# A fourth adding transfer per block in a selective-scan decoder layer, and one product moved from POOL to DVE

## What is computed

```
x = layernorm(x + mamba(x))
x = layernorm(x + cross_attention(x, ctx))
x = layernorm(x + gated_ffn(x))

mamba:  u = silu(conv4(W_in x) + b)           # 1024 channels
        dt, B, C = W_xproj u                  # 16 states
        delta = softplus(W_dt dt + b_dt)
        h_t = exp(delta_t A) h_(t-1) + delta_t B_t u_t   # for each channel and state
        y_t = sum over the 16 states of C_t h_t
        out = W_out ((y + D u) * silu(W_res x))
```

## Time and profile before

| what | value |
|---|---|
| median of 3 runs | 2497.8 us |
| the profiled execution | 2494.77 us |
| its span, first to last instruction | 2493.0 us |
| mamba part in it | up to about 1710 us |
| busy PE, DVE, ACT, POOL, share of the whole span | 93%, 73%, 63%, 67% |
| mean granted TensorE clock | 0.979 |

### The profile page before, as it was taken

One profiled execution on the slowest core, in us unless ns is written; L12 is line 12 of the kernel. 1 busy time (PEld: TensorE's weight loads), 2 busy tenths in 40 slices (PEclk: granted clock), 3 DMA queues, 4 the chain that ended last, 5 costly groups with the idle time before them and its releaser, 6 DMA issues. The chain is left out here.

```text
span 2493.0 us, 38410 instructions
## 1 busy us (share of the span) xinstructions
PE 2328.9 (93%) x15232; PEld 1389.2 (56%) x15232; DVE 1830.0 (73%) x2160; ACT 1566.4 (63%) x2604; POOL 1675.3 (67%) x911
## 2 busy tenths in 40 slices
PE   8898999999999999899999989996799999999997
PEld 4565666566666665566656655563454554554543
DVE  4998898898898899889889878762465366356453
ACT  4786887878888878688788887742333433333332
POOL 1898889899899899789989988871333143143130
PEclk9999999999999999999999999997899999999999
DMA  6677978877878888787787787875000100000000
GB/s 205 142 151 167 223 153 178 216 170 172 219 160 186 207 165 174 163 214 159 168 224 170 167 216 151 209 179 187 1 32 4 34 34 1 34 34 1 17 17 17
DMA packets 104677, 331.67 MB, mean 133 GB/s; under 512 B 9699, under 2 KB 46947, under 8 KB 73779
## 3 DMA queue, kind: packets, MB, share of 16 engines
q0 software_dynamic: 27648, 201.34, 40.9%
q1 hardware_dynamic: 76851, 127.88, 15.1%
HBM read 108.30 MB, written 19.56 MB: 51 GB/s over the span
## 5 line engine op out<-in xcount | busy, mean ns | idle before, releaser
L1028 POOL TENSOR_TENSOR mamba_ring<-mamba_ring,mamba_c_row 128x1024 f32<-128x1024 f32 x512 | 1278.7, 2655 | 39.5 <-DVE mamba_ring L916 39.1
L916 DVE TENSOR_TENSOR_SCAN mamba_ring<-mamba_ring,ps 128x512 f32<-128x512 f32 x1024 | 1175.0, 1200 | 139.8 <-PE ps L456 134.1
L717 ACT ACTIVATE mamba_ring<-mamba_delta,mamba_a_neg 128x512 f32<-128x512 f32 x1024 | 659.4, 710 | 73.5 <-DMA mamba_ring<-mamba_ring 72.1
L456 PEld LDWEIGHTS ps<-shared,mamba_v_t 64*128 64x128 f32 x8192 | 499.5, 189 | 245.1 <-issue 148.1
L456 PE MATMUL ps<-shared,mamba_v_t 64*128 64x128 f32 x8192 | 581.1, 284 | 49.8 <-DVE mamba_ring L916 48.8
L1037 POOL DMA_DIRECT2D mamba_ring<-mamba_ring x192 | 180.3, 939 | 147.6 <-DMA mamba_ring<-mamba_ring 121.8
L1614 POOL TENSOR_TENSOR xf_pr<-xf_pr,xf_top 128x1232 f32<-128x1232 f32 x32 | 75.0, 2344 | 266.4 <-DVE xf_top L1536 266.4
L422 PE MATMUL ps<-mamba_xt,mamba_wres 128*128 128x512 f32 x512 | 239.7, 611 | 0.0
L365 PE MATMUL ps<-mamba_xt,mamba_wu 128*128 128x512 f32 x464 | 218.3, 614 | 5.6 <-DMA mamba_xt<-x_t 5.6
L890 DVE SCALAR_TENSOR_TENSOR mamba_u<-ps,mamba_wcv,mamba_u 128x511 f32<-128x511 f32 (+2 forms) x192 | 142.1, 740 | 74.3 <-ACT mamba_u L682 71.8
L508 PE MATMUL ps<-mamba_wout,mamba_u 128*128 128x512 f32 x352 | 168.0, 611 | 0.3 <-ACT mamba_gate L725 0.3
(11 more groups left out here) (129 smaller groups left out, 2781.7 us busy)
## 6 DMA issues: line engine op xcount, KB each, us to landing
mamba_ring<-mamba_ring POOLq DMA_DIRECT2D x192, 1024.0 KB, 7.7
mamba_c_row<-c_rows SPq DMA_DIRECT2D x32, 1024.0 KB, 11.6
mamba_wres<-w_res SPq DMA_DIRECT2D x64, 256.0 KB, 6.0
mamba_wu<-w_u SPq DMA_DIRECT2D x58, 256.0 KB, 4.0
mamba_xres<-x SPq DMA_DIRECT2D x32, 256.0 KB, 8.9
x<-mamba_xres SPq DMA_DIRECT2D x32, 256.0 KB, 4.4
mamba_xt<-x_t SPq DMA_DIRECT2D x7, 1024.0 KB, 14.2
xf_xn<-x SPq DMA_DIRECT2D x20, 256.0 KB, 4.0
```

Of the source, the lines that this page charges most:

```text
L456: m = nc.tensor.matmul(ps[:, 2 * s + i, tb * P:(tb + 1) * P], v_t[g % 2][i * H:(i + 1) * H, tb * P:(tb + 1) * P], diag_b[i * H:(i + 1) * H ...
L717: a = nc.scalar.activation(ring[:, q % NR, i, :], delta[:, d % EARLY, :], ACT.Exp, scale=a_neg[:, d, 2 * k + i:2 * k + i + 1])
L916: m = nc.vector.tensor_tensor_scan(ring[:, r, i, :], ring[:, r, i, :], both[:, bass.ds(i, T, 2)], 0.0, ALU.mult, ALU.add)
L1028: nc.gpsimd.tensor_tensor(ring[:, q % NR], ring[:, q % NR], c_row[:, 2 * k:2 * k + 2, :], ALU.mult).then_inc(c_done, 1)
```

## The change

A fourth merge of half the size (one slot, 512 KB) adds the slot of step 6 to that of step 7. It is issued after POOL's step 4 of block g + 1 and waits for merge 2. PE's state_sum takes the slot of step 7 alone, and runs at the end of PE's step 7. y_transposes moves to the end of PE's step 0 of block g + 2. v for blocks 6, 7 and the next batch's 0 is made by DVE, behind its scan of step 1 of blocks 5, 6 and 7, and no longer by POOL. ACT's program stays as it is.

```diff
+    LIGHT = 5
-    MERGES = 3
-    SUMS = (6, 7)
+    MERGES = 4
+    SUMS = (7,)
...
     PE step:
-                if k == 6 and g >= 1:
-                    for e in SUMS:
-                        state_sum(g - 1, e)
...
                 if k == 7 and g >= 1:
-                    y_transposes(g - 1)
+                    for e in SUMS:
+                        state_sum(g - 1, e)
+                if k == 0 and g >= 2:
+                    y_transposes(g - 2)
...
+            y_transposes(NG - 2)
...
     DVE:
+            def make_v(g):
+                b, d = g // ND, g % ND
+                dve.wait_ge(delta_ready, g + 1)
+                dve.wait_ge(u_ready, g + 1)
+                dve.wait_ge(vt_proj, g)
+                nc.vector.tensor_tensor(v[:].rearrange("p b i t -> p i b t"), in_blocks(delta[:, d % EARLY, :]),
+                                        in_blocks(u[b % 2][:, d, :]), ALU.mult).then_inc(v_ready, 1)
...
+                if k == 1 and d >= LIGHT and g + 1 < NG:
+                    make_v(g + 1)
...
     POOL merge:
-                src, dst = (g * NU + 2 * p) % NR, (g * NU + 2 * p + 2) % NR
-                pool.wait_ge(c_done, g * NU + 2 * p + 4)
+                n = 2 if p < 3 else 1
+                src, dst = (g * NU + 2 * p) % NR, (g * NU + 2 * p + n) % NR
+                pool.wait_ge(c_done, g * NU + 2 * p + 2 * n)
...
-                nc.gpsimd.dma_start(ring[:, dst:dst + 2], ring[:, src:src + 2], accum_op=ALU.add).then_inc(merged[p], 16)
+                nc.gpsimd.dma_start(ring[:, dst:dst + n], ring[:, src:src + n], accum_op=ALU.add).then_inc(merged[p], 16)
...
     POOL loop:
-                    if k == 0 and g + 1 < NG:
+                    if k == 0 and g % ND < LIGHT:
                         make_v(g + 1)
                     times_c(g * NU + k)
...
                     if k in (3, 6):
                         merge(g, k // 4)
+                    if k == 4 and g >= 1:
+                        merge(g - 1, 3)
             merge(NG - 1, 2)
+            merge(NG - 1, 3)
```

## The result

The changed kernel takes 2768.7 us (median of 4 runs, 2764.8 to 2771.3). The kernel before, on the same chip, takes 2499.1 us. The ratio is 1.109, with a 95% interval of [1.106, 1.111]. So it is 270 us slower. I had said 2640, 142 slower, with 2700 as the upper end: the sign and the place were right, the size was not. In the profiled executions the spans differ by 276.5 us, and the last scan of the mamba part ends at 1940.7 us in place of 1665.4, 275.3 later. What comes behind the mamba part takes 1.2 us more.

A forecast was written before the change was run, and what follows sets the result against it. PE was taken as nearest to a bound, with DVE and ACT as late in some blocks. 2494.8 + 133 + 18 + 5 + 3.5 - 15 = 2639, said as 2640 us; range 2540 to 2700.

The forecast's parts named there:

- The new wait: PE's state_sum waits for merge 3, queued behind merge 0; take_yt comes 14.0 us after the scan of step 3.
- Sum 22.1 us a batch: Lateness of take_yt adds up over a batch's eight blocks, one loop turn each; 133 us for batches 1 to 6.
- its own 512 KB, 2.6: Merge 3's data behind merge 0 on the queue: 2.6 us, half of a 1 MB merge's 5.3.
- 1.0 (8 transposes): PE's sum between merge 3's landing and take_yt: eight transposing matmuls in 1.0 us.
- C: Rival, slower still: 23 make_v on DVE meet a busy POOL and PE's clock falls; 60 us more, 2700; chance 0.10.
- Batch 7 has no taps: 5: In the last batch only the path over PE counts, costing 5 us.
- The blocked make_diags gone, −15: On DVE, the two make_diags held in the kernel before should be held no longer: 15 us less.
- no block for make_v itself: POOL is idle when make_v starts on DVE, so it takes 0.7 us; bounds nothing and 7.5 each.
- Relief of PE: Eight of 16 transposing matmuls less per block: 63 us in all, nothing where DVE or ACT is as late.
- POOL at nothing: POOL's extra transfer issue, 0.94 us per block, and three products less a batch are about level: costed at nothing.
- A: Rival: merge 3 is cheaper, 1.2 us of data or partly beside merge 0; 2580, down to 2540; chance 0.18.
- B: Rival, faster: merge 3 lands before PE reaches the sum, four PE-filled blocks a batch gain 1.0 each; 2449; chance 0.08.

The follow-up runs named there:

- The filled run: The changed kernel with four useless products on PE ahead of the sum's wait for merge 3, in six of eight blocks; 2719.4 us, ratio 1.089.
- The relief of PE alone: The kernel before with the slot of step 6 left out of PE's sum, so eight transposes less per block; 2489.8 us, ratio 0.996.

## Why the prediction went right and wrong

- **The new wait, its place and its mechanism: right.** PE waits for the ring's transfer ahead of the sum, 222.8 us (I named 150 or more). take_yt to the next scan 3 is 13.0 (12.9). Merge 3 lands at 7.8 (7 or more). Merge 0 itself took 8.1, under my mean of 8.6. Issuing merge 3 first brought it down to 5.0, which shows that it waits in the queue.
- **"Sum 22.1 us a batch": failed; two terms were too small.** The stretch from scan 3 to take_yt was forecast at 14.9 in the mean and is 16.56. 1.1 of the 1.6 is "its own 512 KB, 2.6". By the medians of a block that is right in quiet blocks (2.5 in blocks 2 and 3), but where SP loads weights beside it, in blocks 0, 1 and 4, it is 3.6 or 3.7, and in block 7, beside the C rows and x, 7.3. I had given merge 0 of block 7 this surcharge, from the earlier trace rows, and forgotten merge 3, which moves behind it under the same loads. Another 0.6 is "1.0 (8 transposes)": in five of the eight blocks they mostly take 1.9, at the 1.2 GHz level, after the idle stretch that I had forecast myself. Over 48 blocks these 1.6 are 77 us. Batches 1 to 6 took 217 us more than before against a forecast of 133, 84 over, and 94 or so with the blocked make_diag of batch 4, whose loss I had counted apart. The other 17 were not taken apart; some of them will lie where I let lateness vanish: the turn from scan 3 of block 4 to that of block 5 grew by 2.3 us (forecast 0), the next one by 6.3 (2.8), a part of which is in the 1.6 already.
- **The clock: put in the wrong place.** I had it only in the rival of held make_vs (C). It falls with the wait itself, which is 3.9 us in the mean of 57: in the turn shown, 16 matmuls take 1.91 us behind it and 16 of the same 1.16 us later. The filled run prices it at some 50 us or more, part of which is the 0.6 above.
- **"Batch 7 has no taps: 5": failed.** That batch took 240.3 us against 202.5, 38 more. Without taps the loop can close over PE instead: sum, take_yt, transposes back, gate_y, scan. After the change gate_y waits in nearly every block, 307.8 us in all, and DVE's scans stand behind it; no run opened this path alone. I had seen it in block 5 and not asked whether it binds everywhere. PE also waits 9.55 us for a load in block 4 of that batch. Batch 0 took 22 more (18). So the misses are 84, 33 and 4, and 15 for the two blocked make_diags, whose end is contained in these times already; the start of the mamba part and the tail behind it came out 4 under what I had put. Together 132, the miss in the profiled executions (129 by the medians).
- **The blocked make_diags gone, −15, and "no block for make_v itself": right** for the changed kernel. None of 23 was held, and the make_diag behind it took 2.85 (2.7). But v on DVE is not the near-nothing of my sum: it costs 20 us in the changed kernel and 27 where merge 3 is absent.
- **The order on PE: not costed.** It alone is +20 us, as an added step between the sum and those who wait for it.
- **Relief of PE: right in kind** ("where DVE or ACT is as late, it is nothing"): 7 to 13 us of 63.
- **POOL at nothing: right.** As much traffic and the issue without the wait are 7 to 9 us, and POOL waits 360.4 us for DVE.
- **The rivals.** A (cheaper merge 3) and B (faster) failed. The number of C was nearest, but for another cause: no make_v was held.
- **The range** ended at 2700. It took "1.2 to 3.5" for merge 3's data, though I had named 5.3 as the upper bound of this term further up; measured are 3.7 in the mean. And it took in neither the loads beside merge 3 nor the clock at its place; both point the same way and come on together.

No run that computes the whole result was faster than the kernel before. The relief of PE alone was, and leaves a slot out of the sum.

## What to carry to other kernels

A transfer that is added to a loop of waits costs its landing time behind whatever is ahead of it in its queue and beside whatever else moves then, so price it block by block at the loads of that block, and follow the loop through every engine also where the path you looked at first is missing. When a change makes TensorE wait in each turn, price the lower clock of all that it does next as part of that wait. An operation with two SBUF operands on VectorE is safe only where GpSimd idles when it starts; started in the midst of a GpSimd product, it lasts until GpSimd has run out of work that is ready (45 of 45 held make_v here).

## What was unexpected of the hardware

- A DVE product of two SBUF operands took 0.67 us free and 2.8 to 9.0 us held. Whether it was held hung on whether POOL was inside a product at its start, and so on how far POOL was behind: in the changed kernel, where POOL ends its product of step 3 on average 2.6 us behind DVE's scan, none of 23 make_v was held; in the run with merge 3 first, at 4.4 us behind, 15 of 23. Shifting other work moved the hold from make_v to make_diag and back more often than it removed it.
- Useless matmuls in a wait gave 49 us: the clock rose from 0.91 to 0.98 of full in the mamba part.
- On one queue a 512 KB adding transfer landed 4.6 to 6.3 us after its issue when nothing was ahead of it, and 6.8 to 7.9 when a 1 MB one was (medians of blocks 0 to 4); in quiet blocks it landed 2.5 us behind that one. The order in the queue changed who waits, not how long the two take together: 11.8 us from the first issue to the last landing in the changed kernel, and 11.9 with merge 3 first (means of batches 1 to 6).
